# A mixture-of-experts stage: every token through all eight experts, or each through its two, by indirect DMA

## What is computed

```python
def _L0_ffn_ref(x, gate_w, ew1, ew2, ew3, sw1, sw2, sw3):     # EXPERTS = 8, TOP_K = 2, H = 256
    def swiglu(x, w1, w2, w3):
        h = x @ w1
        return h * jax.nn.sigmoid(h) * (x @ w2) @ w3
    top_v, top_i = jax.lax.top_k(x @ gate_w, TOP_K)
    ...                                                       # w: softmax over the two chosen, 0 elsewhere
    out = sum over e of swiglu(x, ew1[e], ew2[e], ew3[e]) * w[..., e]
    return out + swiglu(x, sw1, sw2, sw3)                     # the shared expert, for every token
```

## Time and profile before

| | |
|---|---|
| Median of 3 runs | 3462.02 us (3461.8 to 3464.02) |
| Profiled execution, own time | 3476.31 us |
| Its span, first to last instruction | 3474.5 us |
| PE busy (share of the span) | 3246.8 us (93%) |
| DVE, ACT, POOL busy | 2576.4 (74%), 1731.6 (50%), 1223.6 (35%) |
| Mean granted TensorE clock | 0.975 |
| DMA, mean over the span | 23 GB/s, all on SP's hardware queue |

### The profile page before, as it was taken

One profiled execution on the slowest core, in us unless ns is written; L12 is line 12 of the kernel. 1 busy time (PEld: TensorE's weight loads), 2 busy tenths in 40 slices (PEclk: granted clock), 3 DMA queues, 4 the chain that ended last, 5 costly groups with the idle time before them and its releaser, 6 DMA issues. The chain is left out here.

```text
span 3474.5 us, 92529 instructions
## 1 busy us (share of the span) xinstructions
PE 3246.8 (93%) x28757; PEld 2726.8 (78%) x28882; DVE 2576.4 (74%) x7263; ACT 1731.6 (50%) x5782; POOL 1223.6 (35%) x3404
## 2 busy tenths in 40 slices
PE   6999999788888888999999998999999899999995
PEld 5888888565555555999999997888888778888884
DVE  3777777566666665888888886777777568888887
ACT  3665666355555552222222222777777566666663
POOL 1444444333333331000000001666767434444443
PEclk8999999899999998999999999999999899999997
DMA  3000000111111100000000000000000000000000
GB/s 116 23 23 23 21 23 20 33 33 30 30 30 32 30 24 12 12 11 11 11 11 12 11 11 13 23 21 22 21 20 23 24 22 28 24 27 24 27 20 12
DMA packets 166239, 81.57 MB, mean 23 GB/s; under 512 B 19680, under 2 KB 164448, under 8 KB 166112
## 3 DMA queue, kind: packets, MB, share of 16 engines
q1 hardware_dynamic: 166112, 79.98, 8.1%
HBM read 58.94 MB, written 20.97 MB: 23 GB/s over the span
## 5 line engine op out<-in xcount | busy, mean ns | idle before, releaser
L1660 PE MATMUL psS<-experts_xT,e 128*128 128x256 f32 x2304 | 552.5, 383 | 0.0
L1694 ACT ACTIVATE experts_th<-psS 128x512 f32<-128x512 f32 x288 | 172.0, 597 | 604.0 <-PE psS L1660 604.0
L1660 PEld LDWEIGHTS psS<-experts_xT,e 128*128 128x128 f32 x2304 | 417.4, 191 | 48.2
L1070 ACT ACTIVATE pr<-psS,small 128x128 f32<-128x128 f32 x1024 | 365.0, 386 | 176.8 <-DVE small L1160 150.4
L1424 ACT ACTIVATE pr<-psT 120x1024 f32<-120x1024 f32 (+1 forms) x256 | 262.3, 1025 | 326.2 <-PE psT L1345 326.2
L1469 DVE TENSOR_REDUCE small<-psS 128x4 f32<-128x992 f32 x256 | 303.9, 1188 | 105.2 <-PE psS L1349 103.6
L821 POOL TENSOR_SCALAR pr<-pr,small 128x128 f32<-128x128 f32 (+1 forms) x1024 | 360.3, 374 | 36.4 <-DVE small L764 30.2
L1198 POOL TENSOR_SCALAR self_Qx<-self_qk,headmask 128x128 f32<-128x128 f32 x1024 | 359.8, 382 | 16.9 <-DVE self_qk L1117 16.9
L1335 PE MATMUL psT<-cross_Qm,cross_xf 32*120 32x512 f32 (+1 forms) x1024 | 294.6, 645 | 67.3 <-DVE small L1469 22.3
L1669 PEld LDWEIGHTS psT<-e,experts_gu 128*128 128x128 f32 x2304 | 302.3, 191 | 16.1 <-DVE experts_gu L1782 1.3
L1669 PE MATMUL psT<-e,experts_gu 128*128 128x128 f32 x2304 | 303.6, 275 | 1.1 <-DVE experts_gu L1782 1.1
(11 more groups left out here) (282 smaller groups left out, 7999.9 us busy)
## 6 DMA issues: line engine op xcount, KB each, us to landing
between<-self_xo SPq DMA_DIRECT2D x128, 64.0 KB, 1.6
cross_x<-between SPq DMA_DIRECT2D x128, 64.0 KB, 1.7
cross_res<-between SPq DMA_DIRECT2D x128, 64.0 KB, 1.7
cross_cx<-in_ctx SPq DMA_DIRECT2D x128, 60.0 KB, 1.8
self_x<-in_x SPq DMA_DIRECT2D x64, 64.0 KB, 1.7
self_res<-in_x SPq DMA_DIRECT2D x64, 64.0 KB, 1.7
cross_fs<-in_fside_BxSxS SPq DMA_DIRECT2D x64, 64.0 KB, 1.8
between<-cross_xo SPq DMA_DIRECT2D x64, 64.0 KB, 1.6
```

Source lines behind the costliest of these rows:

```text
L1070: last = act.activation(pr[e.slot % 4][:, cols], K.S[e.slot % 2][:, cols], ACT.Exp, bias=nmax[e.slot % 4][:, n:n + 1], accum_out=tot[k.slo ...
L1660: last = pe.matmul(K.S[u.slot % 2][:, at0 + blk * T:at0 + (blk + 1) * T], w[:, j, blk * P:(blk + 1) * P], xT[i.slot][:], start=True, stop= ...
```

## The change

`experts` is replaced by `experts_sparse`. It keeps all of x in SBUF and works in phases:

1. PE transposes all 64 sequences, ACT copies them, PE computes all gate logits.
2. DVE, with three small matmuls, picks each token's two experts and gives each (token, expert) pair a row in a tensor `slots` of 136 blocks of 128 rows, each block of one expert. `expert` holds the expert of each block.
3. POOL scatters x into `slots` by 128 indirect DMAs of 128 rows each (two per sequence). At the same time PE, ACT and DVE run the shared expert for all pairs.
4. SP loads the 136 blocks; PE transposes each, multiplies it with the weights of the expert whose number it loads into a register, transposes the gated product and multiplies it with `e3`; ACT copies; SP stores to `results`.
5. POOL gathers each token's two result rows by indirect DMA (two per sequence), DVE adds them with their probabilities and normalises.

Rows of `slots` that no token takes must hold numbers, so `set_up` clears all of `slots` with 17 stores of 512 KB of zeros.

```diff
@@ set_up
+        empty = K.slots.rearrange("(p a) d -> p (a d)", p=P)
+        K.EMPTIED = empty.shape[1] // (8 * P)
...
                 for sem, some in ((first_in, first_loads), (w_in, loads), (K.experts_in, expert_loads)):
                     for dst, src in some:
                         sp.dma_start(dst, src, allow_slow_non_contiguous=True).then_inc(sem, 16)
+                sp.wait_ge(halved, 4)
+                for i in range(K.EMPTIED):
+                    sp.dma_start(empty[:, 8 * P * i:8 * P * (i + 1)], K.zeros[:]).then_inc(K.emptied, 16)
@@ experts -> experts_sparse, SP
+                sp.dma_start(route[:], D["c_route"][:, 0:P + 9 * EXPERTS + nblocks]).then_inc(consts_in, 16)
+                for n in range(loads):
+                    sp.dma_start(x[:, 8 * n:8 * n + 8, :], x_eights[n]).then_inc(x_in[n], 16)
...
+                    if a.live:
+                        need(sp, bT_ps, (a - 4).done())
+                        sp.dma_start(xb[a.slot][:], slot_blocks[a.n]).then_inc(xb_in[a.slot], 16)
                     if o.live:
+                        need(sp, ob_sb, o.done())
+                        sp.dma_start(result_blocks[o.n], ob[o.slot][:]).then_inc(kept[o.slot], 16)
+                sp.wait_ge(scattered, 16 * 2 * nseq)
+                pipeline(sp, step, ring, nblocks, *bspan)
@@ PE, one block
+                    if b.live:
+                        e = pe.value_load(expert[0:1, bass.ds(b.n, 1)], min_val=0, max_val=EXPERTS)
+                        need(pe, bT_sb, b.done())
+                        need(pe, bopened, (b - 2).done())
+                        pe.matmul(K.S[b.slot % 2][:, 0:T], xbT[b.slot][:], K.e1[:, bass.ds(e, 1), :].rearrange("p a f -> p (a f)"), start=True, stop=True).then_inc(bh_ps, 1)
+                        need(pe, bgT_sb, (b - 2).done())
+                        pe.matmul(K.S[b.slot % 2][:, 512:512 + T], xbT[b.slot][:], K.e2[:, bass.ds(e, 1), :].rearrange("p a f -> p (a f)"),
+                                  start=True, stop=True).then_inc(bhu_ps, 1)
+                    if g.live:
+                        need(pe, bgated, g.done())
+                        for blk in range(2):
+                            last = pe.transpose(K.S[g.slot % 2][:, 768 + blk * P:768 + (blk + 1) * P],
+                                                bgu[g.slot % 2][:, blk, :], K.ident[:])
+                        last.then_inc(bgT_ps, 1)
+                    if t.live:
+                        e = pe.value_load(expert[0:1, bass.ds(t.n, 1)], min_val=0, max_val=EXPERTS)
...
+                        for blk in range(2):
+                            last = pe.matmul(W[2 + t.slot % 2][:, 0:P], bguT[t.slot % 2][:, blk, :], K.e3[:, bass.ds(e, 1), blk, :].rearrange("p a n -> p (a n)"),
+                                             start=(blk == 0), stop=(blk == 1))
+                        last.then_inc(bout_ps, 1)
@@ POOL
+                pool.wait_ge(placed, 2)
+                pool.wait_ge(K.emptied, 16 * K.EMPTIED)
+                for s in range(nseq):
+                    for k in range(2):
+                        pool.indirect_dma_start(slots, bass.IndirectOffsetOnAxis(idx[k][:, s:s + 1], 0), x[:, s, :],
+                                                None).then_inc(scattered, 16)
+                for i in range(ring):
+                    pool.wait_ge(kept[i], 16 * len(range(i, nblocks, ring)))
+                for i in range(nseq + 3):
+                    s, n = seq(i), seq(i - 3)
+                    if s.live:
+                        need(pool, joined, (s - 4).done())
+                        for k in range(2):
+                            pool.indirect_dma_start(got[k][s.slot][:], None, results,
+                                                    bass.IndirectOffsetOnAxis(idx[k][:, i:i + 1], 0)).then_inc(got_in[s.slot], 16)
```

More of the change, by code:

```diff
@@ L1577, in attend_keys_major, with experts_sparse, pair, seq @@
         K.passed()
-def experts(K, D, tag, x_dram, out_dram, nseq):
+def experts_sparse(K, D, tag, x_dram, out_dram, nseq):
     nc = K.nc
[L1585 to L1592, removed]
+    T = 2 * P
+    pairs = nseq // 2
+    nblocks = 2 * nseq + 8
+    ring = 4
+    loads = nseq // 8
+    x_eights = x_dram.rearrange("(i a) p d -> i p a d", a=8)
+    slots = K.slots
+    slot_blocks = slots.rearrange("(b p) d -> b p d", p=P)
+    results = nc.dram_tensor(tag + "results", [nblocks * P, P], F32, kind="Internal").ap()
+    result_blocks = results.rearrange("(b p) d -> b p d", p=P)
+    def pair(m):
+        return At(m // ring, m % ring, ring, pairs)
+    def seq(s):
+        return At(s // ring, s % ring, ring, nseq)
     K.taken = 0
@@ L1615, in experts @@
[L1615 to L1624, removed]
@@ L1632, in experts @@
-        span = (-units, 2 * uring, (count - 1) // ring * ring * units, ucount + units)
+        grid = [P, nseq, EXPERTS]
+        logits, hits, rank = (sb(n, grid) for n in ("logits", "hits", "rank"))
+        first, second = sb("first", grid), sb("second", grid)
+        both = sb("both", grid, BF16)
+        top, nxt, at, gap, ex, den, p1, p2 = (sb(n, [P, nseq, 1]) for n in (
+            "top", "nxt", "at", "gap", "ex", "den", "p1", "p2"))
+        idx = [sb(f"idx{i}", [P, nseq], U32) for i in range(2)]
@@ new lines, in experts_sparse @@
+        blocks, ends, starts = (sb(n, [P, EXPERTS, 1]) for n in ("blocks", "ends", "starts"))
+        upto = sb("upto", [P, EXPERTS, EXPERTS])
+        past = sb("past", [1, nblocks, EXPERTS])
+        owner = sb("owner", [1, nblocks, 1])
+        expert = sb("expert", [1, nblocks], U32)
+        xb = [sb(f"xb{i}", [P, P]) for i in range(ring)]
+        xbT = [sb(f"xbT{i}", [P, P]) for i in range(ring)]
+        bth = [sb(f"bth{i}", [P, T]) for i in range(2)]
+        bgh = sb("bgh", [P, T])
+        bgu = [sb(f"bgu{i}", [P, 2, P]) for i in range(2)]
@@ L1699, in _ @@
-                pipeline(act, step, uring, ucount, *span)
+                for m in range(pairs):
+                    act.wait_ge(xT_ps, m + 1)
+                    act.copy(xT[:, m * T:(m + 1) * T], W[2 + m % 2][:, 0:T]).then_inc(xT_sb, 1)
+                act.wait_ge(gating, 15)
+                act.activation(ex[:], gap[:], ACT.Exp).then_inc(exped, 1)
+                for m in range(pairs):
+                    act.wait_ge(h_ps, m + 1)
+                    need(act, opened, m - 1)
+                    act.activation(th[m % 2][:], K.S[m % 2][:, 0:2 * T], ACT.Tanh, scale=0.5).then_inc(tanhed, 1)
@@ L1701, in _ @@
+                pipeline(act, step, ring, nblocks, *bspan)
             @block.vector
             def _(dve):
[L1703 to L1714 removed]
@@ L1750, in step @@
[L1750 to L1759 removed]
+                dve.wait_ge(consts_in, 16)
```

421 lines of the change are left out of this document (257 added, 164 removed).

## The result

The changed kernel takes 3487.05 us (median of 7 runs, 3478.76 to 3492.47), the kernel before on the same chip 3464.95 (7 runs, 3461.8 to 3476.62): ratio 1.0053, 95% interval 1.0037 to 1.0068. Forecast was 3427, faster; it came out slower by half a percent, inside the range. The profiled execution took 3481.67 us, against 3476.31 of before.

What follows compares the result with a forecast made beforehand. PE, busy 93% of the span, was taken as the bound. Five phases summed to 731 us against 793.9, 63 less; set-up's 28 left 35 less, so 3441 profiled, 3427 us by the median; range 3290 to 3590.

Steps and rivals of the forecast that it cites:

- POOL's indirect DMA: Scatter and gather: 1.15 us for each of 256 DMAs, about twice POOL's 0.55 us power; the change pays below 1.29.
- the scatter: Phase 3, POOL's 128 indirect DMAs beside the shared expert: 149 us, 147 of issue and 2 for the last landing.
- the gather: Phase 5, after all blocks are stored: 202 us, 64 sequences at 3.04 us of POOL, plus 7 for the last.
- the first rival: Scatter and gather: POOL slower, 1.6 us per indirect DMA, 115 us more, 3542 us in all; chance 0.22.
- Blocks: Phase 4, 136 blocks of expert matmuls: 329 us, at 2.34 us per block plus fill, drain and last store.
- 1.64 + 0.70 = 2.34: Per block in phase 4: 1.64 us of PE matmuls and transposes, plus 0.35 us stall for each of two register loads.
- Gates: Phase 1, transposes and gate matmuls of 32 pairs of sequences: 32 us, at 0.9 us per pair.
- Set-up: Zero stores before the first stage delay the load of self_x: 28 us added, 8.9 MB at 272 GB/s.
- Positions: Phase 2, a chain of dependent DVE operations with two trips to PE: 19 us.
- shared expert: Dense expert run beside the scatter in phase 3: 32 x 2.61 + 3 = 89 us.
- The second rival: Block loop does not keep PE's clock or queue full; at 1.2 GHz 223 us more, 3650 us; chance 0.12.
- The third: Scatter and gather: POOL nearly as quick as SP, 0.4 us per indirect DMA, 3276 us in all; chance 0.18.

Runs made afterwards that it cites:

- experiment 3: Changed kernel with each of the 128 scatters taking 64 rows instead of 128: 3567.72 us in one run.
- experiments 7: Changed kernel with the block loop written out and the expert a constant, so no register load: 3374.41 us in one run, 1.640 us per block.
- experiment 9: Changed kernel, block loop kept, both loads replaced by constant expert 0: 3375.04 us; its sum gives PE's sequencer 1.28 us per block, 0.44 per load, 0.32 for the loop.

## Why the prediction was wrong

The way the time would go was right, phase by phase, with PE's work gone and POOL's queue and stalls in its place. The sign was wrong, because the margin was 35 us and five terms were each off by 10 to 18. In the profiled execution's measure the forecast was 3441. Put in what was measured: 59 more in the expert stage, 10 less in the set-up, 8 less in the first cross stage, gives the 3482 that it took. The other 19 us between the forecast of 3427 and the median of 3487 are no phase: I took off the 14.3 us by which the profile of before lay above its median, and the profile of after lay 5.4 below its own. That the error of the sum stayed at 41 us is partly luck, since the set-up and the cross stage gave back 18.

- **POOL's indirect DMA** is the step that failed. I put "about twice" a power of 128 numbers, 1.15 us; it is 1.293. The step itself named the point from which the change costs: 1.29. At 128 in the scatter the difference is 18 us, nearly the 17.4 that the phase was over; the gather was over by 12.8, since a sequence took 3.26 us instead of 3.04. These 30 us are the largest part of the error, but they alone would have left 5 of the 35 us of margin; the blocks' 18 and the gates' 10, against 10 that the set-up gave back, turned the sign. What I left out was the 0.30 us between two of them, which no row of before could show; the instruction itself, 0.97, was under my figure. The reason that I gave, 128 indices and a descriptor for each row, was wrong too: by experiment 3 the rows cost about 1 ns each, 0.13 us in all, and the rest is paid whatever their number. That the price decides, that issue and landing overlap (a scatter lands after 2.2 us, a gather after 2.6, and the next is issued 1.3 after the last), and that the first rival with 1.6 was too dear, held. The Trainium skill (DMA: Bandwidth & Descriptors, section Anatomy of one DMA, SWDGE path) gives by its fit an estimated 2.15 us for 64 KB. The scatter's landing of 2.2 agrees, the gather's of 2.6 is longer; the fit is of one DMA from issue to completion and not of the time from one issue to the next, so it would have been wrong as a term of the sum.
- **Blocks**, 347 instead of 329, is the second step that failed, and by its mechanism: the sum 1.64 + 0.70 = 2.34 was near 2.487 by luck. The 1.64 held (experiments 7 and 9). The loads do not add to the matmuls; they add to PE's sequencer, which ran beside the matmuls and became the bound. A load is 0.30 us, and 0.44 with what follows it. The Trainium skill (same page, section Latency and other measured facts) gives a tensor_load some 600 ns; here 272 of them took half of that. Had I counted the sequencer's instructions in a block rather than asked how long one matmul waits, I would have had a lane to hold against the 1.64: by the sum of experiment 9 it is 1.28 + 2 x 0.44 + 0.32 = 2.48. The term for the loop I had at nothing.
- **Gates**, 42 instead of 32. A pair took 1.17 us, at a granted clock of 0.50 with PE busy 37.6 of 40 us. My price of 0.9 came from rows at the full clock, where transposes stand 0.11 us apart; here recorded matmuls stand 0.21 to 0.25 apart, and I had no rival in which a busy PE gets the low clock. Four of the six recorded matmuls of a pair move only 8 columns each; that this is why the clock stayed low is not shown.
- **Set-up**, 17.8 instead of 28. The stores moved 419 GB/s, where the loads of the earlier trace rows made 272. I took the rate of loads for stores of another shape.
- **Positions** 19.4 against 19; **shared expert** 86 against 89: right, the shared expert priced from rows of the same shape, the positions partly from them.
- The second rival (PE's clock falls in the block loop) did not occur: 1.00 from 1615 to 1936 at 77% busy. The third, POOL as quick as SP at 0.4 us, was far off: 1.293.

## What to carry to other kernels

Divide the forecast's margin by the number of times its unseen price is paid: here 35 us over 256 DMAs, 0.14 us each on a guess of 1.15, which is too thin for a chance of 0.58 on one side. Where register loads or loops enter an engine's stream, add up its sequencer's time as a second lane beside the array's; what lies under the longer lane is free, and one load fewer was worth more here (0.44 us) than the whole loop (0.32). And work that is spread over phases should be tried by moving it into the phase in which its queue is empty, as with the zeros, and by batching the small instructions of the engine that sets the pace.

## What was unexpected of the hardware

- An indirect DMA costs POOL nearly the same for 64 rows (0.899 us) as for 128 (0.966), plus 0.30 between two.
- PE's clock stayed at the lower level, 0.50, with PE busy 94% of 40 us in transposes and matmuls of 8 columns, and at 1.00 with it busy 77% in the block loop.
- PE's semaphore increments arrived up to 41 us late while POOL issued indirect DMAs, in all four kernels of one job on one chip, and never in the eight runs on others, with the same program in one case. It cost that program 73 us of its expert stage. In the same four traces, and in no other, most increments of the scatters are missing from the record. The cause is open.
